# A graph, attention and expert kernel on one core: attention's operations ahead of the bias and the first subtraction, sums on ScalarE, the router's columns behind the shared w1, a later ranking

## What is computed

```python
# layer 0: x = x + gnn(ln(x)) + linear_attention(ln(x)); x = x + expert_choice_ffn(ln(x))     (8 experts)
xn = layernorm(x)
x = x + relu(diffusion(xn) @ W + b) + attention(xn) @ W_out + b_out      # layer 1
#   attention: q,k,v = xn @ W_qkv; q_phi = elu(q)+1, k_phi = elu(k)+1
#   out = (q_phi @ (k_phi^T @ v)) / (q_phi @ sum(k_phi))  per head
xn = layernorm(x)
gate_out = xn @ gate_w + routing_bias                                    # 16 logits a row
weights = softmax over the 4 largest, 0 elsewhere (ties: the lower number wins)
out = swiglu(xn, sw1, sw2, sw3)                                          # the shared expert
for e in range(16):                                                      # 16 routed experts
    out = out + swiglu(xn, w1[e], w2[e], w3[e]) * weights[:, e:e+1]
x = x + out                      # swiglu(x,w1,w2,w3) = (silu(x @ w1) * (x @ w2)) @ w3, inner width 1365
```

## Time and profile before

| what | us |
|---|---|
| median of 3 runs | 539.53 (539.36 to 540.14) |
| the profiled execution | 539.64 |
| its span from first to last instruction | 537.9 |
| TensorE busy in the span | 523.7 (97%) |
| VectorE busy | 427.3 (79%) |
| ScalarE busy | 334.9 (62%) |
| GpSimd busy | 7.5 (1%) |
| granted clock, mean | 0.994 of full speed |

### The profile page before, as it was taken

One profiled execution on the slowest core, in us unless ns is written; L12 is line 12 of the kernel. 1 busy time (PEld: TensorE's weight loads), 2 busy tenths in 40 slices (PEclk: granted clock), 3 DMA queues, 4 the chain that ended last, 5 costly groups with the idle time before them and its releaser, 6 DMA issues.

```text
span 537.9 us, 7561 instructions
## 1 busy us (share of the span) xinstructions
PE 523.7 (97%) x2674; PEld 406.8 (76%) x2674; DVE 427.3 (79%) x427; ACT 334.9 (62%) x313; POOL 7.5 (1%) x32
## 2 busy tenths in 40 slices
PE   8999899998999999999999999999999999999997
PEld 4665344465878888888888888888888888888885
DVE  6724510267999989899898999989899998989795
ACT  1101100146787778687777878777787877778573
POOL 2000000000100000000000000000000000000000
PEclk9988999999999999999999999999999999999999
DMA  8999999999999999999989999999999999999331
GB/s 339 423 420 422 421 421 421 422 407 416 399 287 418 410 374 327 355 396 339 401 294 372 361 365 376 344 356 329 377 357 362 338 344 403 329 373 347 117 108 68
DMA packets 36745, 190.11 MB, mean 353 GB/s; under 512 B 4059, under 2 KB 4187, under 8 KB 31221
## 3 DMA queue, kind: packets, MB, share of 16 engines
q1 hardware_dynamic: 36528, 189.70, 91.5%
q10 hardware_dynamic: 196, 0.14, 0.1%
HBM read 189.56 MB, written 0.26 MB: 353 GB/s over the span
## 4 chain that ended last, share of the span: by engine, by line
PE 82%; DMA 8%; DVE 7%; issue 1%; ACT 1%; POOL 0%; SPq 0%; DVEq 0%; POOLq 0%
PE ps L1533 29%; PE ps L1571 23%; PE ps L1537 14%; DMA w_set<-in_w 5%; PE ps L1555 4%; DVE s_lo L862 3%; DMA w_raw<-in_sw 2%; PE ps L1192 2%; PE ps L1356 1%; PE ps L1254 1%; DVE s_lo L874 1%; PE ps L1244 1%; PE ps L1373 1%; PE ps L1185 1%; PE ps L1258 1%
## 5 line engine op out<-in xcount | busy, mean ns | idle before, releaser
L862 DVE TENSOR_TENSOR s_lo<-w_raw,s_hi 128x1365 fp32r<-128x1365 f32 x136 | 209.1, 1578 | 13.4 <-ACT s_hi L635 13.0
L635 ACT CAST s_hi<-w_raw 128x1365 fp32r<-128x1365 f32 x136 | 180.5, 1337 | 28.8 <-PE ps L1537 13.2
L1533 PE MATMUL ps<-s_hi,xT_hi 128*128 128x512 f32 (+1 forms) x408 | 153.8, 377 | 0.4 <-DVE s_lo L862 0.2
L1533 PE MATMUL ps<-s_lo,xT_hi 128*128 128x512 f32 (+1 forms) x408 | 149.7, 369 | 0.0
L1537 PE MATMUL ps<-s_hi,xT_lo 128*128 128x512 f32 (+1 forms) x408 | 106.6, 369 | 0.0
L874 DVE TENSOR_TENSOR s_lo<-w_raw,s_hi 128x1536 fp32r<-128x1536 f32 x68 | 105.8, 1578 | 0.0
L647 ACT CAST s_hi<-w_raw 128x1536 fp32r<-128x1536 f32 x68 | 90.8, 1343 | 22.4 <-PE ps L1537 18.3
L1533 PEld LDWEIGHTS ps<-s_hi,xT_hi 128*128 128x128 f32 x408 | 76.6, 188 | 17.4 <-issue 0.9
L1533 PEld LDWEIGHTS ps<-s_lo,xT_hi 128*128 128x128 f32 x408 | 77.0, 189 | 12.5
L1537 PEld LDWEIGHTS ps<-s_hi,xT_lo 128*128 128x128 f32 x408 | 72.6, 189 | 6.0
L1571 PE MATMUL ps<-s_hi,hT_hi 128*128 128x512 f32 (+1 forms) x182 | 73.7, 405 | 0.2 <-DVE hT_lo L1069 0.2
(11 more groups left out here) (239 smaller groups left out, 298.3 us busy)
## 6 DMA issues: line engine op xcount, KB each, us to landing
w_raw<-in_w SPq DMA_DIRECT2D x128, 682.5 KB, 6.4
w_raw<-in_w SPq DMA_DIRECT2D x51, 768.0 KB, 6.2
w_set<-in_w SPq DMA_DIRECT2D x32, 1024.0 KB, 25.1
w_raw<-in_w SPq DMA_DIRECT2D x12, 512.0 KB, 6.4
w_raw<-in_sw SPq DMA_DIRECT2D x8, 682.5 KB, 15.8
wk_sb<-in_wk SPq DMA_DIRECT2D x2, 1024.0 KB, 16.9
wq_sb<-in_wq SPq DMA_DIRECT2D x2, 1024.0 KB, 19.0
gcn_sb<-in_gcn_w SPq DMA_DIRECT2D x2, 1024.0 KB, 13.1
```

Of the source, the lines that this page charges most:

```text
L635: a.copy(s_hi[pair][:, 0:F1], raw[:]).then_inc(hi_ready, 1)
L862: v.tensor_tensor(s_lo[pair][:, 0:F1], raw[:], s_hi[pair][:, 0:F1].bitcast(F32), ALU.subtract).then_inc(lo_ready, 1)
L1533: mm(bank(i + c0 // D)[:, 0:even(n)], xT_hi[:, k], w[:, c0:c0 + even(n)], start=(k == 0 and w is hi), stop=False)
```

## The change

- VectorE: the row sums of W_out leave it; `keep_diagonal` stands ahead of the bias, and all of attention ahead of the first subtraction, which now follows x1's relu; `lo_w1(0, 1)` stands behind x3. The variance of x3 is no longer taken by VectorE from x3 (two statistics passes and their aggregate) but by one small addition to a sum of squares.
- ScalarE: four copies with a sum each give W_out's row sums; exp of q stands behind the first rounding instead of the second; the fourth rounding of w1 behind x1's sum; xT_hi ahead of the first rounding of w2; the copy of x3's transpose is gone; a Square with a sum gives the variance.
- The router's product of 4 matrices of 16 columns in fp32 is gone: GpSimd writes gate_w's high and low part behind the 1366 columns of the shared w1's pairs (8 small instructions), and the last chunk of the shared w1's units is 358 columns wide instead of 342. The logits are read from bank 2 once all four units are done.
- The ranking has three operations ahead of its reduction instead of four and stands behind the second subtraction of expert 1; the first h stands behind the fourth subtraction instead of the second. On TensorE the first transposes of the shared expert's h stand behind the third w1 unit of expert 1 instead of the second.
- The last quarter of the graph product is done in two halves of 256 columns, the second behind the first transposes of mix. The mean of layer 1's x takes one two-column product instead of two one-column ones.

The core of the diff (semaphore names, the new slices and the mean's products left out):

```diff
@@ -537,6 +540,12 @@
 
             pool.wait_ge(ffn0_ps, 2)
             clear_pads(range(4))
+            pool.wait_ge(ld_small, 16)
+            for k in range(KT):
+                hi, lo = s_hi[pair_of_w1(0, k)][:, GATE], s_lo[pair_of_w1(0, k)][:, GATE]
+                pg.tensor_copy(hi, gate1_w[:, k]).then_inc(gate_parts, 1)
+                pool.wait_ge(gate_parts, 2 * k + 1)
+                pg.tensor_tensor(lo, gate1_w[:, k], hi.bitcast(F32), ALU.subtract).then_inc(gate_parts, 1)
             pool.wait_ge(q_ps, 2)
             clear_pads(range(4, 5))
             pool.wait_ge(gnn1_ps, 1)
@@ -665,27 +674,34 @@
             copy_v(1)
             act.wait_ge(zT_ps, 1)
             a.copy(zT[:], tiles(0)).then_inc(zT_ready, 1)
+            act.wait_ge(ld_wout, 16)
+            for k in range(KT):
+                if k > 1:
+                    act.wait_ge(wout_sum_ready, k - 1)
+                a.activation((xn, gnn)[k % 2][:], wout_sb[:, k, 2:2 + D], ACT.Copy, accum_out=wout_sum[:, k]).then_inc(wout_sum_ready, 1)
             hi_w1(0, 0)
+            exp_q(1)
             hi_w1(0, 1)
-            exp_q(1)
             hi_w1(0, 2)
-            hi_w1(0, 3)
 
             for b in range(2):
                 act.wait_ge(mixT_ps, 1 + b)
                 a.copy(mixT[:, HALF_T[b]], mix_halves[b]).then_inc(mixT_ready, 1)
             act.wait_ge(x1_ready, 1)
-            a.activation(neg_q[:], x1[:], ACT.Copy, accum_out=x1_total).then_inc(x1_total_ready, 1)
+            act.wait_ge(wout_sum_ready, KT)
+            a.activation(xn[:], x1[:], ACT.Copy, accum_out=x1_total).then_inc(x1_total_ready, 1)
+            hi_w1(0, 3)
+            for b in range(2):
+                act.wait_ge(xnT_ps, 5 + b)
+                a.copy(xT_hi[:, HALF_T[b]], half_tiles(3, b)).then_inc(x_hi_ready, 1)
+            act.wait_ge(xn_ready, 6)
+            act.wait_ge(x1_total_ready, 1)
+            a.activation(xn[:], x3[:], ACT.Square, scale=D ** -0.5, accum_out=x3_squares).then_inc(squares_ready, 1)
             act.wait_ge(q_ps, 2)
             act.wait_ge(k_ps, 2)
             hi_w2(0, 0)
-            for b in range(2):
-                act.wait_ge(xnT_ps, 5 + b)
-                a.copy(xT_hi[:, HALF_T[b]], half_tiles(3, b)).then_inc(x_hi_ready, 1)
             act.wait_ge(v_ps, 2)
             act.wait_ge(gnn1_ps, 1)
-            act.wait_ge(x_lo_ready, 2)
-            a.copy(xnT[:].rearrange("p (b t) n -> p b t n", b=2), both_halves(3)).then_inc(xnT_ready, 1)
             hi_w2(0, 1)
             hi_w2(0, 2)
             hi_w2(0, 3)
@@ -1014,13 +1031,10 @@
             dve.wait_ge(rstd_ready, 3)
             v.tensor_scalar(scaled_polyT, polyT[:], rstd[:], None, ALU.mult).then_inc(scaled_poly_ready, 1)
             scaled_keys()
-            dve.wait_ge(ld_wout, 16)
-            v.tensor_reduce(wout_sum, wout_sb[:, :, 2:2 + D], AX_X, ALU.add).then_inc(wout_sum_ready, 1)
+            keep_diagonal(1)
             dve.wait_ge(x2_ready, 2)
             dve.wait_ge(ld_l1_rows, 16)
             then(v.tensor_tensor(x1[:], x2[:], bout_all[:], ALU.add))
-            lo_w1(0, 0)
-            keep_diagonal(1)
             negative_q(1)
             phi_q(1)
             attended_half(0)
@@ -1028,7 +1042,7 @@
             dve.wait_ge(gnn1_ps, 1)
             v.scalar_tensor_tensor(x1[:], bank(1), 0.0, x1[:], ALU.max, ALU.add).then_inc(x1_ready, 1)
             dve.wait_ge(x1_ready, 1)
-            lo_w1(0, 1)
+            lo_w1(0, 0)
 
 
             dve.wait_ge(x1_total_ready, 1)
@@ -1040,13 +1054,14 @@
                 v.scalar_tensor_tensor(x3[:, HALF[b]], wout_halves[b][:, 1 - b:1 - b + D // 2], minus_mean3, x1[:, HALF[b]],
                                        ALU.add, ALU.add).then_inc(xn_ready, 1)
             v.memset(h[:, F1:even(H_COLS)], 0.0)
+            lo_w1(0, 1)
             for b in range(2):
                 dve.wait_ge(x_hi_ready, b + 1)
                 v.tensor_tensor(xT_lo[:, HALF_T[b]], half_tiles(3, b), xT_hi[:, HALF_T[b]].bitcast(F32),
                                 ALU.subtract).then_inc(x_lo_ready, 1)
             lo_w1(0, 2)
-            dve.wait_ge(xn_ready, 6)
-            halves_variance([x3[:, half] for half in HALF])
+            dve.wait_ge(squares_ready, 1)
+            v.tensor_scalar(var_eps[:], x3_squares, LN_EPS, None, ALU.add).then_inc(var_ready, 1)
             lo_w1(0, 3)
 
             def gated(e, kind, carries):
@@ -1081,10 +1096,9 @@
 
                 other = logits1[:].unsqueeze(1).to_broadcast([P, E1, E1])
                 own = logits1[:].unsqueeze(2).to_broadcast([P, E1, E1])
-                v.tensor_tensor(rank_t[0][:], other, own, ALU.is_gt)
-                then(v.tensor_tensor(rank_t[1][:], other, own, ALU.is_equal))
-                then(v.tensor_tensor(rank_t[1][:], rank_t[1][:], below16[:], ALU.mult))
-                then(v.tensor_tensor(rank_t[0][:], rank_t[0][:], rank_t[1][:], ALU.add))
+                then(v.tensor_tensor(rank_t[0][:], other, own, ALU.subtract))
+                then(v.scalar_tensor_tensor(rank_t[1][:], rank_t[0][:], 0.0, below16[:], ALU.is_ge, ALU.mult))
+                then(v.scalar_tensor_tensor(rank_t[0][:], rank_t[0][:], 0.0, rank_t[1][:], ALU.is_gt, ALU.max))
                 then(v.tensor_reduce(rank1[:], rank_t[0][:], AX_X, ALU.add))
                 dve.wait_ge(exp1_ready, 1)
                 w = weights1[:, 1:1 + E1]
@@ -1098,15 +1112,13 @@
             router_max()
             lo_w2(0, 2)
             lo_w2(0, 3)
-            router()
 
             def body(e, kind, carries):
                 for k in range(KT):
-                    if k == KT // 2 and isinstance(e, int) and e == 1:
-                        gated(0, kind, carries)
                     lo_w1(e, k)
-                if not (isinstance(e, int) and e == 1):
-                    gated(e - 1, kind, carries)
+                    if k == 1 and isinstance(e, int) and e == 1:
+                        router()
+                gated(e - 1, kind, carries)
                 lo_w3(e - 1, 0, kind)
                 if isinstance(e, int) and e == 1:
@@ -1482,18 +1493,17 @@
             keys_values(1)
             project_q(wq1_sb, xsT, range(KT // 2, KT))
 
-            def diffused(ks):
+            def diffused(ks, cols=slice(0, D)):
 
                 for k in ks:
-                    last = mm(bank(1), zT[:, k], gnn_w_sb[:, k], start=False, stop=(k == KT - 1))
-                if KT - 1 in ks:
-                    last.then_inc(gnn1_ps, 1)
+                    last = mm(bank(1)[:, cols], zT[:, k], gnn_w_sb[:, k, cols], start=False, stop=(k == KT - 1 and cols == HALF[1]))
+                return last
 
             pe.wait_ge(ld_gnn_w, 16)
             pe.wait_ge(zT_ready, 1)
             diffused(range(3))
             attend(1)
-            diffused(range(3, KT))
+            diffused(range(3, KT), HALF[0])
 
             def transpose_mix(b):
                 pe.wait_ge(mix_ready, 2 + b)
@@ -1511,8 +1521,9 @@
                     last.then_inc(wout_ps, 1)
 
             transpose_mix(0)
+            diffused(range(3, KT), HALF[1]).then_inc(gnn1_ps, 1)
             pe.wait_ge(ld_wout, 16)
-            pe.wait_ge(wout_sum_ready, 1)
+            pe.wait_ge(wout_sum_ready, KT)
             pe.wait_ge(mixT_ready, 1)
             project_out(0, range(2))
             transpose_mix(1)
                     for w in (hi, lo):
-                        mm(bank(i + c0 // D)[:, 0:even(n)], xT_hi[:, k], w[:, c0:c0 + even(n)], start=(k == 0 and w is hi), stop=False)
+                        mm(bank(i + c0 // D)[:, 0:n], xT_hi[:, k], w[:, c0:c0 + n], start=(k == 0 and w is hi), stop=False)
                 if isinstance(g, int) and g in (0, 2):
                     pe.wait_ge(x_lo_ready, g // 2 + 1)
-                for c0, n in CHUNK:
-                    last = mm(bank(i + c0 // D)[:, 0:even(n)], xT_lo[:, k], hi[:, c0:c0 + even(n)], start=False, stop=(k == KT - 1))
+                for c0, n in chunks:
+                    last = mm(bank(i + c0 // D)[:, 0:n], xT_lo[:, k], hi[:, c0:c0 + n], start=False, stop=(k == KT - 1))
                 last.then_inc(used, 1)
 
             def up_w1(e, k):
@@ -1572,23 +1585,22 @@
                 last.then_inc(used, 1)
 
             pe.wait_ge(pads, 2 * PAIRS_N)
+            pe.wait_ge(gate_parts, 2 * KT)
             pe.wait_ge(x_hi_ready, 1)
             for k in range(KT):
                 up_w1(0, k)
-                if k == 1:
-
-                    pe.wait_ge(xnT_ready, 5)
-                    for j in range(KT):
-                        last = mm(bank(7)[:, 0:E1], xnT[:, j], gate1_w[:, j], start=(j == 0), stop=(j == KT - 1))
-                    last.then_inc(gate1_ps, 1)
             for k in range(KT):
                 up_w2(0, k)
 
             def body(e, kind):
                 up_w1(e, 0)
                 up_w1(e, 1)
-                transpose_h(e - 1, 0, kind)
-                up_w1(e, 2)
+                if isinstance(e, int) and e == 1:
```

(15 more changed lines are left out.)

23 lines of the change are left out of this document (12 added, 11 removed).

## The result

The changed kernel takes **537.43 us** (median of 6 runs, 537.00 to 538.67); the kernel before, run beside it, 539.66 (539.36 to 540.14). The ratio is 0.9954, with a 95% interval of 0.994 to 0.9969: 2.2 us faster. The forecast was 537.2, with a range of 536.3 to 538.5. The profiled execution took 537.37 (span 535.6) against 539.64. TensorE's granted clock is 0.57 in the mean from 34 to 38 us, as before, and 1.00 from 100 us to the end.

What follows compares the result with a forecast made beforehand. Bound: VectorE's chain from 119 to 160 us, then TensorE to the end. Attention's earlier start and VectorE's terms sum to -2.31: 539.64 - 2.31 = 537.3, median 537.2; own range 536.7 to 537.8, stated range 536.3 to 538.5.

Steps and rivals of the forecast that it cites:

- the -2.31 of the sum: Start of attention to the shared expert's second chunk on VectorE: -1.96 - 0.43 + 1.50 - 1.08 - 0.34 = -2.31 us.
- Part 1: Attention starts at 121.8, 1.96 us earlier, then limited by TensorE's graph product; x3 follows at 127.7.
- Part 2: ScalarE's four row sums of W_out take 2.5 to 3.3 us from 115.4 and cost nothing before exp of q.
- Part 3: VectorE, x3 to second chunk: xT_hi wait -0.43, lo_w1(0, 1) +1.50, statistics -1.08, ranking -0.34 us.
- Part 4: Logits behind the fourth shared w1 unit: units end at 137.3, VectorE arrives at 137.5, a cover of 0.2 us.
- if VectorE waits for the logits: One of the signs listed as showing the prediction wrong: VectorE waiting at the logits' read, expected near 137.5.
- The product gone is worth nothing: The router's own product on TensorE (0.96 us at 135.37) goes, but TensorE has time there: worth nothing.
- The wait for h: TensorE waits a new 0.8 us for h near 150.6; free, since VectorE's path stays the later by 0.2.
- clock rival: Two rivals: TensorE's clock falls in one stretch near 150.6 (538.9, chance 0.04) or in two (540.6, chance 0.03).
- A shorter VectorE would be worth at most 0.2: At the second chunk, VectorE's and TensorE's paths lie 0.2 us apart, so less VectorE work gains at most that.
- The rest a copy of before, shifted: After the second chunk at 157.6 the program repeats the kernel before, shifted; from 160 us TensorE alone counts.
- GpSimd: Eight new instructions from 108 on, 0.55 to 1.81 us each, end near 112.6 to 122.7, before 129.6.

Runs made afterwards that it cites:

- e11: Changed kernel with the last quarter of the graph product whole again behind attention's product, instead of split in halves: 537.57 us.
- e12: Kernel before with VectorE's order alone changed (keep_diagonal ahead of the bias, first two subtractions later) and exp of q ahead of the second rounding: 539.20 us.
- e2: Changed kernel with W_out's row sums again one reduction on VectorE and ScalarE's four copies with sums taken out: 537.15 us.
- e3: Changed kernel with the variance of x3 again from VectorE's statistics instead of ScalarE's Square and one addition: 538.14 us.
- e5: Changed kernel with the router's own fp32 product back, GpSimd's eight column operations and the wider products out: 537.24 us.
- e4: Changed kernel with the ranking and the first h (with its transposes) back at their old places: 537.40 us.
- e7: Changed kernel with the logits one subtraction later on VectorE and the first h between expert 1's third and fourth subtraction: 537.08 us.
- e6: Changed kernel with the logits one subtraction later on VectorE, behind lo_w2(0,2): 537.39 us.
- e1: Changed kernel with the shared expert's first subtraction back ahead of attention, between the bias and keep_diagonal: 540.36 us, ratio 1.0008 to the kernel before.
- e8: Changed kernel with the last expert's w3 units 1 to 3 loaded early, into the space of w1's raw buffer: 537.06 us.
- e10: Changed kernel with the router's own product back, first h between third and fourth subtraction, and last expert's w3 in w1's raw space: 536.79 us, ratio 0.9938.

## Why the prediction was right

The mechanism held: attention's start was late by what stood ahead of it on VectorE, and VectorE's work set the fifth tile. That the number came so close is in part luck. Up to the fifth tile more was gained than the -2.31 of the sum (2.55; 2.47 from the graph product), and the end took 0.29 of it back (C).

- **Part 1, attention at 121.8, a gain of 1.96.** It started at 121.69, 2.07 earlier; the limit was TensorE's graph product, as said. x3 came 2.30 earlier instead of 1.96. Of the difference of 0.34, 0.11 are attention's start, 0.15 the split of the graph product (e11), which the prediction had down as a delay of x1's relu and not as a gain for the transposes, and 0.08 attention's product without a pause ahead of it. ScalarE's fourth rounding, given no price, adds nothing to this over before; left in its old place it would have cost 0.46 (6.31 in e12, 5.85 in e11).
- **Part 2, the sums: 2.5 to 3.3, free.** They took 2.47 and were free. That they were no gain either (e2) the prediction's terms imply, since attention's limit was TensorE.
- **Part 3, VectorE's terms.** From x3 to the three subtractions it took 132.32 - 127.39 = 4.93, where the terms gave 5.27 from before's 5.28. The signs are right and the sizes off by 0.34: `lo_w1(0, 1)` steps by 1.43 and not 1.50 (128.68 to 130.11), the small addition by 0.06 and not 0.16 (132.26 to 132.32), `xT_lo` by 0.66 for 0.76 in before, and the zeroing of h's tail ahead of them by 0.05 for 0.12. The ranking gave 2.78 for 3.11, the 0.34 said. e3 confirms the statistics' term.
- **Part 4, the logits' cover of 0.2: the mis-sized term.** VectorE arrived at 136.87, not 137.5, and the four units ended 0.34 later. So one of the prediction's own signs of being wrong came, "if VectorE waits for the logits". Both gains above (0.31 earlier at x3, 0.34 less work) met this wait, and "what exceeds it is paid in full" was the right rule. "The product gone is worth nothing" was too kind: the columns cost 0.43 (e5).
- **The wait for h: 0.8 near 150.6, free.** It was 0.91 up to 151.23, and free (e4, e7). The clock stayed full, so neither clock rival came.
- **"A shorter VectorE would be worth at most 0.2": wrong.** It was worth 0.43 in e5. The 0.2 were the distance between VectorE's path and a path over TensorE that starts with a wait for h; but h is VectorE's work too, so a shorter VectorE ahead of h moves both. That e6 gave only 0.23 has the other cause named there.
- **The rest a copy of before, shifted: the step that failed.** The shift was 2.55 at 157 us and 2.26 at the end. In after, e1, e2, e4, e5, e7 and e11, ScalarE waited for the third w3 tile, TensorE paused, and from that rounding's start to VectorE's xn it is 8.66 to 8.68: there the landing sets the end. In before it is 8.66 too and the pause hardly 0.1 (C 374.72, where e3, e8 and e10 have 374.61 or 374.62); the prediction read from it that TensorE alone counts from 160 us on. Against the fifth tile the rounding started at 366.06 in before, 366.34 in after, 367.09 in e1 and 365.92 in e3. The transfer was issued at 360.08 to 360.14 in all of them and took 5.9 in before and e12, 5.8 in e3, 7.0 in e1, and 6.2 or 6.3 in after, e2, e4, e5, e7 and e11. So the change did not delay the issue. Why the transfer takes 0.3 longer in these six is open.
- **GpSimd.** The eight instructions took 0.20 to 0.22 each, far under the 0.55 taken as the cheap end; the root took 0.55 beside a memset of VectorE and 1.81 again beside a subtraction. The Trainium skill ("GPSIMD Engine Reference", Key points) speaks of contention with VectorE instructions that read two SBUF inputs; the trace agrees for the root. The eight are no test of it, as VectorE stood idle from 108.19 to 110.33.

```profile
107.28 0.55 POOL L526 TENSOR_TENSOR rstd<-var_eps,neg_half 128x1 f32<-128x1 f32 x1 [58.01 <-DVE var_eps L797]
...
108.05 0.20 POOL L546 CAST s_hi<-small_sb 128x16 fp32r<-128x16 f32 x1
108.34 0.21 POOL L548 TENSOR_TENSOR s_lo<-small_sb,s_hi 128x16 fp32r<-128x16 f32 x1
...
132.48 1.81 POOL L526 TENSOR_TENSOR rstd<-var_eps,neg_half 128x1 f32<-128x1 f32 x1 [8.19 <-DVE var_eps L1064]
```

## What to carry to other kernels

Move to the front what another engine waits for, and then count what the move pushes into the next stretch: the order alone gave 2.0 at attention and 0.8 at the fifth tile, and what filled it up came from small edits. Of the 1.68 between e12 and after in B, 0.74 are the statistics less the wait for the logits (e3) and 0.15 the split (e11); some 0.46 for ScalarE's rounding and 0.33 for the ranking are read from rows and were not tried alone. Work taken off an engine inside its idle time is worth nothing (the sums), and a product saved on an engine with slack can cost time through the later moment at which its result is read (the router). A wait also moves work on another engine: in e6 later logits made a rounding late behind their exp. And a shift can be lost far away: look at the last loads of the program, whose buffers come free late, and give them room (e8).
